# A scan stage whose states go to PSUM and whose product with C stands directly behind each scan

## What is computed

```python
delta = softplus(einsum('bld,dr->blr', x, W_delta) @ W_dt + b_dt)
Bm = einsum('bld,dn->bln', x, W_B);  Cm = einsum('bld,dn->bln', x, W_C)
A = -exp(A_log)                                   # (256 channels, 16 states)
dA = exp(delta[..., None] * A);  dBx = delta[..., None] * Bm[:, :, None, :] * x[..., None]
# over time t, for every channel and each of the 16 states:
h = dA_t * h + dBx_t;   y_t = sum over n of h[..., n] * C_t[n]
return y + D * x
```

## Time and profile before

| | us |
|---|---|
| median of 3 runs | 1365.47 |
| lowest, highest | 1364.45, 1366.08 |
| span of the profiled execution, first to last instruction | 1362.8 |
| busy: VectorE, TensorE, GpSimd, ScalarE | 904.0, 1039.0, 649.3, 574.8 |

### The profile page before, as it was taken

One profiled execution on the slowest core, in us unless ns is written; L12 is line 12 of the kernel. 1 busy time (PEld: TensorE's weight loads), 2 busy tenths in 40 slices (PEclk: granted clock), 3 DMA queues, 4 the chain that ended last, 5 costly groups with the idle time before them and its releaser, 6 DMA issues. The chain is left out here.

```text
span 1362.8 us, 20764 instructions
## 1 busy us (share of the span) xinstructions
PE 1039.0 (76%) x6769; PEld 921.1 (68%) x6769; DVE 904.0 (66%) x2041; ACT 574.8 (42%) x1282; POOL 649.3 (48%) x591
## 2 busy tenths in 40 slices
PE   4767878778787775776567764699999999999940
PEld 3656767767676774665215653699999888888840
DVE  6999999999999984887986664233232232323218
ACT  3768787787878653443404441121121212111100
POOL 4887888878788832000003555334434344434310
PEclk8999999999999997555778796799999999999985
DMA  8544646465555622123030111788778788888629
GB/s 238 194 137 134 182 146 188 152 186 166 169 172 157 183 59 57 31 43 51 33 123 32 40 40 32 259 275 268 267 259 268 268 274 272 274 271 269 238 75 348
DMA packets 163531, 232.62 MB, mean 171 GB/s; under 512 B 34380, under 2 KB 87996, under 8 KB 162656
## 3 DMA queue, kind: packets, MB, share of 16 engines
q1 hardware_dynamic: 145808, 207.79, 48.7%
q0 software_dynamic: 11280, 19.06, 4.2%
q10 hardware_dynamic: 6336, 4.44, 1.0%
HBM read 203.08 MB, written 23.95 MB: 167 GB/s over the span
## 5 line engine op out<-in xcount | busy, mean ns | idle before, releaser
L1011 PE MATMUL st_y_ps<-ident,st_hc 128*128 128x128 f32 x2048 | 274.0, 292 | 113.9 <-DVE st_hc L530 113.9
L1011 PEld LDWEIGHTS st_y_ps<-ident,st_hc 128*128 128x128 f32 x2048 | 255.5, 203 | 136.5 <-DVE st_hc L530 135.6
L413 POOL TENSOR_TENSOR st_u<-st_dx,codes 128x1024 f32<-128x1024 f32 x127 | 296.5, 2360 | 40.9 <-DVE st_h L522 31.9
L522 DVE TENSOR_TENSOR_SCAN st_h<-st_da,st_u 128x512 f32<-128x512 f32 x256 | 297.7, 1204 | 0.8 <-ACT st_da L749 0.8
L2203 PE MATMUL mo_h<-mo_xt,w 128*128 128x128 f32 (+17 forms) x2048 | 281.1, 288 | 1.9 <-DVE mo_xt L2300 1.9
L2203 PEld LDWEIGHTS mo_h<-mo_xt,w 128*128 128x128 f32 x2048 | 270.4, 192 | 6.7 <-issue 2.7
L2306 DVE TENSOR_TENSOR mo_inter<-mo_silu,mo_h 128x128 f32<-128x128 f32 (+17 forms) x256 | 75.7, 304 | 281.2 <-ACT mo_silu L2277 217.1
L2144 POOL DMA_INDIRECT outs<-mo_o,choice x95 | 93.7, 986 | 232.6 <-DVE mo_o L2317 219.4
L2277 ACT ACTIVATE mo_silu<-mo_h 128x128 f32<-128x128 f32 (+17 forms) x256 | 71.7, 290 | 311.8 <-PE mo_h L2203 210.9
L749 ACT ACTIVATE st_da<-st_delta,st_a_neg 128x510 f32<-128x510 f32 x256 | 171.7, 685 | 57.2 <-DVE st_h L522 52.8
L530 DVE TENSOR_TENSOR st_hc<-st_h,st_cps 128x1024 f32<-128x1024 f32 x128 | 152.7, 1193 | 0.0
(11 more groups left out here) (359 smaller groups left out, 1416.4 us busy)
## 6 DMA issues: line engine op xcount, KB each, us to landing
codes<-bc SPq DMA_DIRECT2D x256, 256.0 KB, 3.8
w<-in_L_ffn_w_dram SPq DMA_DIRECT2D x128, 512.0 KB
wo<-in_L_ffn_wo_dram SPq DMA_DIRECT2D x64, 512.0 KB
co_got<-outs SPq DMA_DIRECT2D x16, 512.0 KB, 6.0
wave<-dist SPq DMA_DIRECT2D x16, 274.0 KB
x<-in_x_dram SPq DMA_DIRECT2D x8, 512.0 KB, 9.2
st_cx<-in_ctx_dram SPq DMA_DIRECT2D x8, 512.0 KB, 4.1
dist<-st_dd SPq DMA_DIRECT2D x32, 128.0 KB, 3.6
```

Of the source, the lines that this page charges most:

```text
L413: nc.gpsimd.tensor_tensor(u_sb[k % URING][:, :, :], dx[p % 2][:, :, :], over_chunks(b_sb[k % BRING]), ALU.mult).then_inc(u_ok, 1)
L522: nc.vector.tensor_tensor_scan(h_sb[k % HRING][:, dh, :], da_ps[dh][:, :], u_sb[k % URING][:, dh, :], 0.0, ALU.mult, ALU.add).then_inc(h_o ...
L1011: m = nc.tensor.matmul(y_ps[t // 2][:, t % 2, dh * P:(dh + 1) * P], hc_sb[k % RING][:, dh, t * P:(t + 1) * P], K.ident[:, :], start=False, ...
```

## The change

`h_sb` and its ring are gone; the scans write into one PSUM tensor `h_ps` with room for both chunks, in the place of the two banks `c_ps`. `take_c` is gone; `times_c` reads the C row in SBUF, so it waits for the row's DMA, and `load_c` waits for the product that last read the slot. In the main loop `scans(k)` stands directly ahead of `times_c(k)`, instead of `scans(k + 1)`. With one `h_ps`, `scans(k)` waits for `hc_ok` of step k-1. At the end of the stage the last transposes and copies use `h_ps` where they used `c_ps`.

```diff
-        h_sb = [sb(f"st_h{i}", [P, DC, PT]) for i in range(HRING)]
-        c_ps = [ps(f"st_cps{i}", [P, PT]) for i in range(2)]
+        h_ps = ps("st_h", [P, DC, PT])
...
             def load_c(k):
                 p, n = divmod(k, N)
                 if k >= CRING:
-                    sp.wait_ge(c_ok, k - CRING + 1)
+                    sp.wait_ge(hc_ok, k - CRING + 1)
...
             def scans(k):
                 dve.wait_ge(u_ok, k + 1)
-                if k >= HRING:
-                    dve.wait_ge(hc_ok, k - HRING + 1)
+                if k >= 1:
+                    dve.wait_ge(hc_ok, k)
                 for dh in range(DC):
                     dve.wait_ge(da_ok, k * DC + dh + 1)
-                    nc.vector.tensor_tensor_scan(h_sb[k % HRING][:, dh, :], da_ps[dh][:, :], u_sb[k % URING][:, dh, :],
+                    nc.vector.tensor_tensor_scan(h_ps[:, dh, :], da_ps[dh][:, :], u_sb[k % URING][:, dh, :],
                                                  0.0, ALU.mult, ALU.add).then_inc(h_ok, 1)
...
             def times_c(k):
                 dve.wait_ge(h_ok, k * DC + DC)
                 if k >= RING:
                     dve.wait_ge(summed, k - RING + 1)
-                dve.wait_ge(c_ok, k + 1)
-                nc.vector.tensor_tensor(hc_sb[k % RING][:, :, :], h_sb[k % HRING][:, :, :],
-                                        over_chunks(c_ps[k % 2][:, :]), ALU.mult).then_inc(hc_ok, 1)
+                dve.wait_ge(c_in[k % CRING], k // CRING * 16 + 16)
+                nc.vector.tensor_tensor(hc_sb[k % RING][:, :, :], h_ps[:, :, :],
+                                        over_chunks(c_sb[k % CRING]), ALU.mult).then_inc(hc_ok, 1)
...
-                if real(p) and k + 1 < NP * N:
-                    scans(k + 1)
+                if real(p) and k:
+                    scans(k)
                 if real(p):
                     times_c(k)
...
-            def take_c(k):
-                act.wait_ge(c_in[k % CRING], k // CRING * 16 + 16)
-                if k >= 2:
-                    act.wait_ge(hc_ok, k - 1)
-                nc.scalar.activation(c_ps[k % 2][:, :], c_sb[k % CRING], ACT.Copy).then_inc(c_ok, 1)
...
                 if real(p) and k + 1 < NP * N:
                     decay(k + 1)
-                    take_c(k + 1)
```

More of the change, by code:

```diff
@@ L173, in states @@
     BRING = CRING = 4
-    URING, HRING, RING = 4, 3, 2
+    URING, RING = 4, 2
     WARM = 32
@@ L251, in states @@
         c_in = [sem(f"st_c_in{i}") for i in range(CRING)]
-        c_ok, u_ok, da_ok, h_ok, hc_ok, summed = (
-            sem("st_" + x) for x in ("c_ok", "u_ok", "da_ok", "h_ok", "hc_ok", "summed"))
+        u_ok, da_ok, h_ok, hc_ok, summed = (
+            sem("st_" + x) for x in ("u_ok", "da_ok", "h_ok", "hc_ok", "summed"))
         ctx_in = [sem(f"st_ctx_in{u}") for u in range(2)]
@@ L828, in _ @@
                     decay(0)
-                    take_c(0)
                 if real(p) and k + 1 < NP * N:
                     decay(k + 1)
-                    take_c(k + 1)
                 a, d = real(p + 1), real(p - 1)
@@ L895, in _ @@
                 act.wait_ge(d_mm, p * 2)
-                nc.scalar.activation(st_sb[:, h, :], c_ps[h][:, :], ACT.Copy).then_inc(st_ok, 1)
+                nc.scalar.activation(st_sb[:, h, :], h_ps[:, h, :], ACT.Copy).then_inc(st_ok, 1)
             take_d(p, 0)
@@ L1058, in _ @@
                 for h in range(2):
-                    m = nc.tensor.transpose(c_ps[h][:, t * P:(t + 1) * P], s_sb[:, t, h * P:(h + 1) * P], K.ident[:, :])
+                    m = nc.tensor.transpose(h_ps[:, h, t * P:(t + 1) * P], s_sb[:, t, h * P:(h + 1) * P], K.ident[:, :])
                     if t == PTT - 1:
```

## The result

The changed kernel takes 1410.56 us (median of 4 runs, 1409.65 to 1412.31) against 1364.96 for the kernel before (1362.88 to 1366.08): a ratio of 1.0337, 95% interval 1.0323 to 1.0352. It is 45.6 us slower; 36.0 were forecast. The profiled execution spans 1409.1 us against 1362.8. VectorE's first instruction of the next stage starts at 574.83 instead of 530.19, so 44.6 us of the loss are in the changed stage; the stages behind it take 834.3 and 832.6 us.

The account below looks back on a forecast made before the run. VectorE's instruction list was taken to bound the changed stage. 14.7 + 18.5 + 4.2 - 0.8 - 0.6 = 36.0 us more gave a span of 1398.8 and a time of 1401.5 us; 8 in 10 range 1388 to 1413.

Parts of the forecast that it names:

- PSUM target: Scans writing h into PSUM instead of SBUF: taken as zero cost, bounded by 9 us less and 11.5 us more.
- whole: At VectorE's step 10, whole newly waits 0.6 us for ScalarE's exponential, seven times: 4.2 us more.
- Scan to product: times_c waits for the scan directly ahead, wait written first, short gap: 0.115 us more in 128 steps, 14.7 us.
- Product to scan: scans wait for the product directly ahead, wait written second: 1.193 + 0.105 - 1.11, 0.185 us in 100 steps, 18.5 us.
- The ends: Gains at the stage's start (no wait for a decay, 0.8 us) and end (fewer matmuls ahead, 0.6 us).
- Covers: Later C and B row loads and ScalarE's decays cost nothing; a C row has over 13 us, lands within 8.6.
- (b): Rival: a wait on the neighbour on VectorE costs nothing, only 2.8 us remain, time 1368.3; 4 in 100.
- (a): Rival: PSUM as the scans' target is dearer, 11.5 us more, 1413, or 1417.5 with the product's 4.5; 9 in 100.
- (c): Rival: the scan runs quicker into PSUM, 131 us less if its pace halved, time 1270; 3 in 100.
- (e): Rival: a C or B row comes late directly in front of VectorE; a handful give 1405 to 1415; 2 in 100.
- (d): Rival: TensorE's clock drops, the product waits for summed some 0.7 us a step, up to 1490; 3 in 100.

Follow-up runs that it names:

- e4: The kernel before with only the order changed, scans(k) directly ahead of times_c(k); SBUF h and ScalarE's C copies stay: 1341.28 us against 1315.09, ratio 1.0199.
- e6: The kernel before, order and rings kept, but the product reads the C row in SBUF and ScalarE's copies are gone: 1438.43 us against 1364.97, ratio 1.0529.
- e1: The changed kernel with the wait for hc_ok written ahead of the wait for u_ok in scans: 1355.12 us against 1315.09 for the kernel before, ratio 1.0299.
- e5: The changed kernel with the product cut in two halves, each instruction needing the one two ahead: 1381.87 us against 1364.97 for the kernel before, ratio 1.0132.
- e8: The kernel before with its last neighbour waits on VectorE parted, the product placed between helper halves, two products moved at the ends: 1362.08 us against 1364.97, ratio 0.9974.

## Why the prediction came out as it did

The direction, the cause and the range were right; the size was short by 9.6 us, of which 8.6 lie in the stage. That 1410.56 still fell inside the range was partly luck: the upper end, 1413, was room for a dearer PSUM target, and what filled it was `whole` and the product's own time.

*Scan to product*: forecast 0.115 a step, measured 2.38 - 2.25 = 0.13, 16.6 us for 14.7. The rest is the PSUM target, which I had put at zero.

*Product to scan*: forecast 0.185, measured 1.317 - 1.113 = 0.204 in the mean, 20.4 us for 18.5. The mis-sized step is "1.193 + 0.105 - 1.11". The 1.193 is from a product that does not wait; the one that waits is recorded with 1.22 and takes 0.025 to 0.03 longer from start to start, which also adds 0.6 us in the 20 steps with other work than `whole`. The earlier trace rows had it: start to start 1.26 of a product that waits, against 1.11 in the earlier trace rows. I read the 1.23 there as the price of operands in SBUF, which e4 (1.22 with one operand in PSUM) and e6 (1.20 with both in SBUF, where the product is not held) show to be wrong. The gap was 0.09, not 0.105. That the place of the wait among others sets it, e1 shows.

*whole*: forecast 0.6 us, seven times, 4.2; measured 3.05 - 1.83 = 1.22, 8.5 us. This is the term that was mis-sized most. The wait for the exponential came as forecast: `whole` starts 1.70 after the product where it could have at 1.14, 0.56 us. But it is not what is paid: e4 has it 0.52 us longer and `lost` starts no later. The step that failed is "the other helpers on the two engines move the favourable way, since VectorE's work of step n now comes earlier against ScalarE's and GpSimd's": earlier against GpSimd put `whole` beside GpSimd's product, where before GpSimd stood waiting for `lost`. A sign of it was in the trace of before, in the opening, where small VectorE instructions that start beside GpSimd's one memset end only when it does, at 9.45:

```profile
2.05 7.40 POOL L472 MEMSET wave<- 128x8768 f32 x1
...
7.32 2.15 DVE L550 TENSOR_SCALAR st_near<-st_mv 128x4 f32<-128x4 f32 x1
```

The Trainium skill states it (page "SBUF — State Buffer", section "Who interferes with whom"): VectorE and GpSimd share one pair of ways into SBUF; a VectorE instruction in a two-port mode, which the kind of `whole` can enter, needs the pair, and whichever of the two issues first keeps it to its end; a VectorE instruction with two SBUF inputs contends with a GpSimd instruction that reads SBUF. The runs agree in what they show: 0.68 becomes 1.32 us in `whole`, 1.19 becomes 1.54 in the mean in e6's products, and in e6 the one that clearly starts first is the one that is not held. In which mode `whole` ran no run shows.

*The ends*: forecast 0.8 and 0.6, measured 0.8 and 0.65. Sum by measured terms: 16.6 + 20.4 + 0.6 + 8.5 - 1.45 = 44.7, against 44.6 by the stage's end. The cause of the 1.7 us of the span that lie behind the stage stays open.

*Covers*: the C and B rows came in time (no wait of VectorE names them), ScalarE's decays too.

*Rivals*: (b), that a neighbour's wait is free, is refuted by e5 against the changed kernel, 28.5 us in the stage. (a), the dearer PSUM target, is real at 1.9 us, not 11.5, and at none where the scan's end is not waited for (e5). (c) and (e) did not occur. (d) did not reach VectorE: TensorE's granted clock was 0.88 to 0.95 in the stage's windows from 40 us on, and VectorE's product has no idle time ahead of it but the 0.035 of each step.

## What to carry to other kernels

On an engine that is busy throughout, count the time from start to start, not the recorded lengths. Here the next instruction starts about 0.08 us before the end of one that it does not wait for, and a wait for the direct neighbour takes that overlap away and adds a gap, 0.12 to 0.2 us each. Keep a producer and its consumer one instruction apart, if need be by cutting one of them in two, and where that can't be had write the wait for the neighbour first. When an instruction moves in its own engine's order, look also at what the other engines are doing at its new place: `whole` doubled in length beside GpSimd's product. And before work is taken off an engine because it looks spare, ask where its result lies: here a copy into PSUM was what kept two engines from holding each other up.

## What the runs showed of the hardware that was not expected

- The gap behind a neighbour depends on where its wait stands among several: 0.09 us as the second, 0.03 as the first (changed kernel and e1).
- The same product on the same operands is recorded with 1193 ns in before and with 1221 after a wait for its neighbour in e4. But the record alone says little: in e8 it is 1221 in the mean too, mostly without such a wait, and the starts stand 3.36 us apart as before. What the recorded length follows stays open.
- `whole` beside GpSimd's product ends 0.55 us after that product, whether it could start 0.76 or 0.25 us before the product's end (changed kernel, e4).
- A product with two SBUF operands beside GpSimd's product: both engines slow down, 1193 to 1543 and 2360 to 2967 ns in the mean, and it is the one that starts second that is held, as far as their starts can be told apart (e6).
